# Four chained triangle blocks on one core: the norm's centring in 64x64 quarters with a third x buffer, a table load moved, a last chunk squared by tiles

## The reference

```
xn    = layer_norm(gn(x)) over the 64 channels, with scale and bias
left  = sigmoid(xn @ Wlg + blg) * (xn @ Wl + bl)      # times a mask in layers 0 and 2
right = sigmoid(xn @ Wrg + brg) * (xn @ Wr + br)
out   = einsum over one position axis: 'bikc,bjkc->bijc' (layers 0, 2) or 'bkic,bkjc->bijc' (1, 3)
gate  = sigmoid(xn @ Wog + bog)
result = (layer_norm(out) * gate) @ Wo + bo           # layers 0, 1
result = (layer_norm(out) @ Wo + bo) * gate           # layers 2, 3
```

## Time and profile before

| | us |
|---|---|
| runs: median (lowest, highest of 3) | 2204.35 (2202.63, 2204.5) |
| profiled execution: its time | 2199.82 |
| profiled execution: its span | 2197.9 |

### The profile page before, as it was taken

The page is one execution under the profiler, slowest core; times in us unless marked ns, Lnnn a source line. Parts: engine busy times, 40 slices in busy tenths (PEclk is TensorE's granted clock), DMA queues, the critical chain, the costliest instruction groups (busy, mean ns, idle before and its releaser), DMA issues. The chain is left out here.

```text
span 2197.9 us, 44344 instructions
## 1 busy us (share of the span) xinstructions
PE 1957.8 (89%) x13973; PEld 1352.7 (62%) x13980; DVE 1691.4 (77%) x2690; ACT 1589.8 (72%) x2186; POOL 623.3 (28%) x590
## 2 busy tenths in 40 slices
PE   5798979689898998989989899899998989899998
PEld 4434959555433777865633598886553357778665
DVE  6688898989588767788958897877775877677664
ACT  3588878779788655658978785776887866566676
POOL 0100828265200000026410280742871000000655
PEclk8899999999999999999999999999999999999999
DMA  9488937279788928269979973927997884663897
GB/s 394 162 264 286 281 95 212 90 290 371 256 263 261 335 77 296 87 225 398 410 229 277 273 185 127 276 57 259 402 393 225 274 305 159 219 215 125 296 350 301
DMA packets 430385, 549.47 MB, mean 250 GB/s; under 512 B 15664, under 2 KB 326960, under 8 KB 413872
## 3 DMA queue, kind: packets, MB, share of 16 engines
q1 hardware_dynamic: 428672, 538.38, 72.4%
q10 hardware_dynamic: 1584, 9.51, 1.1%
HBM read 371.67 MB, written 176.16 MB: 249 GB/s over the span
## 5 line engine op out<-in xcount | busy, mean ns | idle before, releaser
L1619 POOL TENSOR_TENSOR LR<-LR 128x512 f32<-128x512 f32 x128 | 186.6, 1475 | 523.3 <-DVE LR L1665 506.4
L823 PE MATMUL bank<-whigh,kept 128*128 128x128 f16 x2048 | 269.4, 231 | 30.5 <-DMA kept<-XH 24.6
L823 PEld LDWEIGHTS bank<-whigh,kept 128*128 128x128 f16 x2048 | 262.0, 150 | 34.7 <-issue 28.1
L1610 POOL TENSOR_TENSOR LR<-LR,sum 128x2048 f32<-128x2048 f32 x30 | 136.5, 4550 | 503.9 <-DVE LR L1427 503.9
L679 PE MATMUL bank<-LR,cen 128*128 128x512 f32 x512 | 254.8, 623 | 22.3 <-DMA LR<-XT 11.2
L823 PE MATMUL bank<-wlow,kept 128*128 128x128 f16 x2048 | 268.5, 231 | 0.0
L823 PEld LDWEIGHTS bank<-wlow,kept 128*128 128x128 f16 x2048 | 262.3, 150 | 0.0
L686 PE MATMUL bank<-LR,kst 128*128 128x512 f32 x512 | 240.9, 593 | 5.2 <-ACT LR L707 5.2
L886 POOL TENSOR_TENSOR msgs<-sigs,mask_sb 128x256 f32<-128x256 f32 x192 | 125.5, 667 | 383.8 <-ACT sigs L860 377.8
L1516 PEld LDWEIGHTS bank<-kst,LR 128*128 128x128 f32 x1024 | 151.4, 193 | 111.9 <-issue 92.5
L1528 PE MATMUL bank<-LR,wog 128*128 128x512 f16 x768 | 213.0, 387 | 6.1 <-ACT msgs L1569 5.3
(11 more groups left out here) (188 smaller groups left out, 4201.6 us busy)
## 6 DMA issues: line engine op xcount, KB each, us to landing
kept<-XH SPq DMA_DIRECT2D x128, 512.0 KB, 5.6
LR<-XT SPq DMA_DIRECT2D x64, 1024.0 KB, 9.6
kept<-XHA SPq DMA_DIRECT2D x128, 512.0 KB, 5.0
LR<-XT SPq DMA_DIRECT2D x112, 512.0 KB, 5.1
XT<-LR SPq DMA_DIRECT2D x56, 1024.0 KB, 8.8
LR<-XH SPq DMA_DIRECT2D x64, 512.0 KB, 7.0
LR<-XHA SPq DMA_DIRECT2D x64, 512.0 KB, 5.9
OS<-kept SPq DMA_DIRECT2D x12, 2048.0 KB, 7.6
```

What stands on the lines that cost most here:

```text
L823: last = pe.matmul(bank(g)[:, j * P:(j + 1) * P], tokens(h, g // 4, g % 4, j, slice(0, P)), w[:, half * P:(half + 1) * P], start=part == 0 ...
L1610: pool.tensor_tensor(v, v, token(sum2, c, C), ALU.mult).then_inc(normalized.s, 1)
L1619: pool.tensor_tensor(by_b(x_of(c), q) if end else by_token_cols(x_of(c), q), by_token(gated[t % 4]), by_token_cols(xi[c % len(xi)], q), AL ...
```

## The change

**Layout.** The two halves of the positions are no longer interleaved: partition 64 s + c. The constants, the entry's copy, the finish's output columns and the end's copy follow.

**Centring.** Each of the two 128x128 matmuls of a tile becomes two of 64x64 by 512 columns: rows by s, output partitions by half of the chunk, the four of a tile on the four quarters of PE's array. A centred tile then holds (half, channel) on the partitions and s in the columns.

**Around it.** A third x buffer (in `obuf[1]`) and loads three chunks on; three `sq` buffers instead of two, three `rs` instead of four. The halving adds 1024 to every row (a tensor-scalar add to f16, then a scalar-tensor-tensor for the remainder), so that all 64 channels are kept and POOL's constant rows go; the weights' folding subtracts the mean instead of dropping a channel. The store of a chunk is eight DMAs in layers 0 and 2, four in 1 and 3.

**Elsewhere.** The sigmoid's table is loaded in the second contraction, behind the Ln and Exp at e = 11, and no longer at the head of the finish. The finish's last chunk is squared in four instructions of 512 columns, and the sums have three more entries.

The diff, cut to its core:

```diff
         def store_xh(sp, n, part, buf, k_is_b, stored_):
-            if k_is_b:
-                for s in range(2):
-                    sp.dma_start(XH[bass.ds(n // 8, 1), 2 * s + (part ^ s), :, :, bass.ds(n % 8, 1), :]
-                                 .rearrange("o c v g f -> (o c) v (g f)"), xh_cols(buf[s::2, :], k_is_b)) \
+            for t in range(2):
+                rows = buf[C * t:C * t + C, :].rearrange("p (s f) -> p s f", s=2)
+                if k_is_b:
+                    for s in range(2):
+                        sp.dma_start(XH[bass.ds(n // 8, 1), 2 * s + (part ^ s), :, 4 * t:4 * t + 4, bass.ds(n % 8, 1), :]
+                                     .rearrange("o c v g f -> (o c) v (g f)"),
+                                     rows[:, s, :].rearrange("p (v f) -> p v f", v=4)).then_inc(stored_.s, 16)
+                else:
+                    blocks = slice(0, 4, 3) if part == 0 else slice(1, 3)
+                    sp.dma_start(XHA[blocks, :, t, bass.ds(8 * n, 8), :].rearrange("s c j a -> c s (j a)"), rows) \
                         .then_inc(stored_.s, 16)
...
+        xt_chunks = [flat[:, (4 + h) * COLS:(5 + h) * COLS] for h in range(2)] + [obuf[1][:, COLS:2 * COLS]]
...
-                        dve.tensor_copy(e_x[n % 2].rearrange("p (v c s) -> p s v c", s=2, c=C),
+                        dve.tensor_copy(e_x[n % 2].rearrange("p (v s c) -> p s v c", s=2, c=C),
...
-            sq, yc, lnv, rs = ([ar.take(GW) for _ in range(k)] for k in (2, 2, 2, 4))
+            sq, yc, lnv, rs = ([ar.take(GW) for _ in range(k)] for k in (3, 2, 2, 3))
...
+                load_xt_chunk(sp, 2, 2, k_is_b)
+                for n in range(NCH - 1):
+                    if n + 3 < from_dram:
+                        sp.wait_ge(centered.s, centered.n + 2 * n + 2)
+                        load_xt_chunk(sp, n + 3, n % 3, k_is_b)
+                    if n >= 1:
+                        store(n - 1, (n - 1) % 2)
...
                 def center(t):
...
-                    for u in range(2):
-                        at = 2 * (t % 2) + u
-                        cols = xa[h][:, at * BANK:(at + 1) * BANK] if k_is_b else \
-                            xa[h].rearrange("p (g j r) -> p j g r", g=16, j=8)[
-                                :, 4 * (at % 2):4 * (at % 2) + 4, 8 * (at // 2):8 * (at // 2) + 8, :]
-                        to = banks[t % 3][:, u * BANK:(u + 1) * BANK]
...
-                        last = pe.matmul(to, cen[:, :], cols, start=True, stop=True)
+                    for half in range(2):
+                        for s in range(2):
+                            rows = slice(C * s, C * s + C)
+                            to = banks[t % 3][C * half:C * half + C, s * BANK:(s + 1) * BANK]
...
+                            elif k_is_b:
+                                cols = xa[h][rows, (2 * half + u) * BANK:(2 * half + u + 1) * BANK]
...
+                            last = pe.matmul(to, cen[rows, rows], cols, start=True, stop=True)
                     last.then_inc(centered.s, 1)
...
-                for t in range(tiles + 1):
-                    if t < tiles:
-                        center(t)
-                    if t > 0:
-                        vary(t - 1)
+                center(0)
+                center(1)
+                for t in range(tiles):
+                    vary(t)
+                    if t + 2 < tiles:
+                        center(t + 2)
...
-                for h in range(2):
-                    pool.memset(high[h][96:P, :], X_SCALE).then_inc(rows_set.s, 1)
-                    pool.memset(low[h][96:P, :], 0.0).then_inc(rows_set.s, 1)
...
-                    dve.scalar_tensor_tensor(yc[t % 4][0:kept, :], banks[t % 3][0:kept, :], cb[0:kept, :],
-                                             rs[t % 4][0:kept, :], ALU.add, ALU.mult).then_inc(normed.s, 1)
+                    dve.scalar_tensor_tensor(yc[t % 4], banks[t % 3][:, :], cb, rs[t % 3], ALU.add, ALU.mult).then_inc(normed.s, 1)
...
-                    dve.tensor_copy(high[h][0:kept, cols], yc[t % 4][0:kept, :]).then_inc(highs_ready.s, 1)
+                    dve.tensor_scalar(to, y, X_SCALE, None, ALU.add).then_inc(highs_ready.s, 1)
                     dve.wait_ge(highs_ready.s, highs_ready.n + t + 1)
-                    dve.tensor_tensor(low[h][0:kept, cols], yc[t % 4][0:kept, :], high[h][0:kept, cols],
-                                      ALU.subtract).then_inc(lows_ready.s, 1)
+                    dve.scalar_tensor_tensor(rest, y, X_SCALE, to, ALU.add, ALU.subtract).then_inc(lows_ready.s, 1)
...
                         root(act, 0)
+                        act.preload_act_table_set("sigmoid_and_others")
...
                 def square(t):
                     c, q = divmod(t, 4)
-                    if q < 3:
-                        return
+                    if c == NCH - 1:
+                        act.wait_ge(x_ready.s, x_ready.n + t + 1)
+                        act.wait_ge(stats_taken.s, stats_taken.n + c + q)
+                        act.activation(pair_cols(squares_out[:, :], q), pair_cols(x_of(c), q), ACT.Square, bias=shift,
+                                       accum_out=stats[:, c + q, 1:2]).then_inc(stats_taken.s, 1)
+                    elif q == 3:
...
-                act.preload_act_table_set("sigmoid_and_others")
...
+    same_side = np.arange(P)[:, None] // C == np.arange(P)[None, :] // C
...
+    k[:, K_CENTER:K_CENTER + P] = np.eye(P) - same_side / C
...
+    k[:, K_MEAN:K_MEAN + P] = same_side / C
...
+    k[:C, K_DROP:K_DROP + P] = (np.arange(C)[:, None] == np.arange(P)[None, :] % C) - 1 / C
+    k[:, K_LAST:K_LAST + P] = 1 / C
```

More of the change, by code:

```diff
@@ L175, in bank @@
             return banks[i // 2][:, (i % 2) * BANK:(i % 2 + 1) * BANK]
-        loaded = [sem(f"loaded{i}") for i in range(2)]
+        loaded = [sem(f"loaded{i}") for i in range(3)]
         landed = [sem(f"landed{i}") for i in range(4)]
@@ L195, in build @@
         normed = sem("normed")
-        rows_set = sem("rows_set")
         highs_ready = sem("highs_ready")
@@ L405, in rest @@
                 for part, w in enumerate((whigh, wlow)):
-                    dve.tensor_tensor(wog[part][:, :].rearrange("p (h s) -> p h s" if late else "p (s h) -> p h s", s=2),
+                    dve.tensor_tensor(wog[part][:, :].rearrange("p (s h) -> p h s", s=2),
                                       w[:, 256:320].unsqueeze(2).broadcast_to([P, C, 2]),
@@ L418, in build @@
         ar = Arena(6 * COLS)
-        e_n = xt_chunks + [ar.take(COLS) for _ in range(2)]
+        e_n = xt_chunks[0:2] + [ar.take(COLS) for _ in range(2)]
         e_x = [ar.take(COLS) for _ in range(2)]
@@ L622, in norm @@
             cb, k_is_b = small[:, 7:8], layer["k_is_b"]
-            per, tiles = 64, 2 * NCH
-            kept = P - 2
+            per, tiles = 128 if k_is_b else 64, 2 * NCH
             @block.sync
@@ L634, in _ @@
                     sp.wait_ge(stored[h].s, stored[h].n)
[L636 to L639, removed]
                 def store_entered(c):
                     sp.dma_start(pair_chunk(XT, c // 8, c % 8), entered(c)).then_inc(stored[2].s, 16)
[L644 to L653, removed]
+                load_xt_chunk(sp, 2, 2, k_is_b)
[5 more added lines that the diff above has]
+                        store(n - 1, (n - 1) % 2)
+                    if from_dram <= n + 2 < NCH:
+                        store_entered(n + 2)
                 for h in range(2):
@@ L699, in square @@
                     act.wait_ge(centered.s, centered.n + t + 1)
[L700 to L701 removed]
+                    act.wait_ge(variance.s, variance.n + t - 2)
+                    act.activation(sq[t % 3], banks[t % 3][:, :], ACT.Square, bias=cb).then_inc(squared.s, 1)
                 def root(t):
@@ L709, in root @@
                     act.wait_ge(logged.s, logged.n + t + 1)
-                    act.wait_ge(normed.s, normed.n + t - 3)
-                    act.activation(rs[t % 4], lnv[t % 2], ACT.Exp, scale=-0.5).then_inc(rooted.s, 1)
+                    act.wait_ge(normed.s, normed.n + t - 2)
+                    act.activation(rs[t % 3], lnv[t % 2], ACT.Exp, scale=-0.5).then_inc(rooted.s, 1)
                 for h in range(4):
                     act.wait_ge(stored[h].s, stored[h].n)
-                for t in range(tiles + 1):
-                    if t < tiles:
-                        square(t)
-                    if t > 0:
-                        root(t - 1)
-            @block.gpsimd
-            def _(pool):
-                for h in range(4):
-                    pool.wait_ge(stored[h].s, stored[h].n)
-                for h in range(2):
-                    pool.memset(high[h][96:P, :], X_SCALE).then_inc(rows_set.s, 1)
-                    pool.memset(low[h][96:P, :], 0.0).then_inc(rows_set.s, 1)
+                square(0)
+                for t in range(tiles):
+                    if t + 1 < tiles:
+                        square(t + 1)
+                    root(t)
             @block.vector
```

72 lines of the change are left out of this document (32 added, 40 removed).

## The result

The changed kernel takes 2176.76 us (median of 4 runs, 2175.5 to 2179.66) where the kernel before takes 2203.65 beside it: a ratio of 0.988, 95% interval 0.9863 to 0.9897. So 27 us are saved where 45 were forecast. The profiled execution took 2175.5 (span 2173.6), 24.3 less than the one before.

What follows compares the result with a forecast made beforehand. It took a ring of waits in the norm, 7.31 of 7.44 us a pair, as the bound. Savings of 37 (norm pairs) + 6 (starts) + 1 (squares) + 1 (table load) = 45 us gave 2159 us, range 2140 to 2250.

Steps and rivals of the forecast that it cites:

- Centring: In the norm: the four quarters run together, so a centring takes 0.86 us, plus 0.18 for the change of array depth.
- the switch: In the norm on PE: changing between 128 and 64 array rows costs 0.18 us each way, at centring and variance product.
- the ring: In the norm: the loop of waits through PE, ACT and DVE for two tiles, falling from 7.31 to 6.71 us.
- Rival A: In the centring: a waiting second pass blocks the next quarter, eight passes take five pass times; 2247 us, chance 0.34.
- rival B: In the centring: only halves of the rows overlap, eight passes take four pass times; about 2204 us, chance 0.10.
- Waits for loads: In the norm: waits for x loads add 0.13 us a pair on average, kept in the forecast pair of 6.84.
- Three x buffers: In the norm: loads start one chunk earlier; alone worth at most 8 us, counted as nothing in the forecast.
- Stores: In the norms of layers 0 and 2: SP's issues take 5.9 us a pair, under 6.84, so the queue keeps up.
- Rival C: In the norm: quarters run together, but DVE's add or SP's eight stores limit pairs to 7.1-7.4 us; 2187 us, chance 0.10.
- Starts: At the norm's start in each layer: shorter first centrings at the lower clock save 1.5 us each, 6 in all.
- Squares: At the finish's last chunk: squaring by tiles on ACT lets three go earlier and saves 1 us.
- Table load: Moved from the finish's head into the contraction: ACT's wait for PE covers its 1.28 us, gaining 1 us.

Runs made afterwards that it cites:

- Experiment 3: The changed kernel with the centring as four matmuls of 128 rows x 64 columns, so only the columns are split: 2221.21 us.
- 10: The changed kernel with the two loops over the quarters exchanged, so neighbours in issue order lie on the same rows and different columns: 2174.88 us.
- experiment 7: The kernel before with the third x buffer alone: 2196.91 us, ratio 0.9968.
- experiment 2: The changed kernel with two x buffers as before, all else kept: 2226.39 us, 1.0096 of the kernel before.
- experiment 1: The changed kernel, layers 0 and 2: x chunks loaded in one DMA instead of two, stores of layer 0's entered x issued from ACT's queue: 2175.98 us.

## Why the prediction was right, and where it was not

The direction and the mechanism held, the size did not: 27 of 45 us.

*Centring*: right. 1.04 with the switch was forecast, 1.02 measured; the ring 6.71, and 6.71 is the pair in the steady parts of layers 1 and 3. That the ring comes out to the hundredth is luck in part: the variance product, 2.02 from its start to the Ln instead of 1.92, shows 0.10 of the 0.18 for the switch back, and the centring starts 1.43 after the scaling instead of 1.33, which no term held. The reason given (neighbours on different rows) was too narrow: experiments 3 and 10 show that halves of the columns overlap as well, and that the order is free. Rival A falls with the four passes at once, rival B with 1.02 instead of 1.7. Experiment 3, where PE is the bound, also bears out the price taken for a change of shape, 0.18 forecast, 0.16 and 0.19 seen.

*Waits for loads*: the 0.13 that I kept were not there with the third buffer (6.70 instead of 6.84 a pair in layers 1 and 3).

*Three x buffers*: "at most 0.13 x 62 = 8 us" is right for the kernel before, where experiment 7 gives 7.9 in the norms. As a price of this part of the change it was wrong: without it the changed kernel loses 50 us and is slower than the one before. I had noted that x loads stand behind stores, but not that x was only just in time already, 9.6 us after its buffer was free, and that a shorter pair and stores that land in 4.1 instead of 2.7 would make it late. That layers 1 and 3 "keep their four" stores said nothing of what each of them costs in the new layout.

*Halving on DVE*: right, 0.685 for the add against the 0.68 taken.

*Stores*: the step that failed. "8 x 0.63 + 2 x 0.44 = 5.9 per pair, under 6.84, so the queue keeps up, with 0.9 to spare" took an issue's price from a queue with room. In the rows above one of eight takes 5.57 / 8 = 0.70 in layer 2 and 6.75 / 8 = 0.84 in layer 0, an x load's 1.19 / 2 = 0.60 instead of 0.44, and 0.75 for a store was named as the point from which SP binds. Rival C's second half thus came true in part of two layers out of four: pairs of 7.10 and 6.94 on average, which cost (7.10 + 6.94 - 2 x 6.70) x 15.5 = 10 us against layers 1 and 3. The same norm sum as forecast is two errors that cancel.

*What no step held*: the late stores stand in front of the projection's first load. The gaps grew by 11.1 us, and nothing in the sum asked what comes next on SP's queue when the norm ends. With four stores the norms and gaps together improve by another 15 us and the kernel takes 2155.4, where I forecast 2159 by a sum in which the stores were free.

*Starts*: first centring to first Ln is 1.5, 1.7, 1.1 and 0.2 shorter, 4.5 instead of 6. *Squares*: 0 instead of 1, since the four tiles queue behind the former chunk's square (the prediction named this queue, but took off only 0.4 for it). *Table load*: 1.8 and 1.4 gained in the finishes of layers 2 and 3, 1.4 lost ahead of layer 1's, so about 1 to 2 where 1 was forecast, but the claim that ACT's wait for PE covers the load is false in layer 1.

What stays open: why eight DMAs of 128 KB hold the queue longer than four of 256 KB with the same bytes and pieces. Taking other issues off SP did not help; what an issue waits for, the profile does not show. Nor is it known why the new layout's stores land later, or how much of the 50 us of experiment 2 is theirs. Nor is it settled how much of the 4.7 us in the projections is the late loads and how much the clock.

## What to carry to other kernels

Price a DMA issue by the queue it will stand in after the change, not by its median in a queue with room; twice as many DMAs for the same bytes is a cost of its own. When a stage is shortened, look at the queue that feeds the next one: what was finished in the shadow of the stage is now in front of the next stage's first load. And a buffer that is worth 8 us in the old kernel can be worth 50 in the changed one, so a part costed at nothing has to be costed with the others made.

## What was not expected of the hardware

A matmul's pass on free columns starts while an earlier one in the code's order waits for its own (641.47, two passes within 0.02 us, columns 0, 0, 1, 1). The same store DMA's issue took 0.66 alone in its queue and 0.92 beside a transfer from another engine's queue, with SP doing nothing else (5.26 / 8 and 7.39 / 8, experiment 1). A store of 256 KB in as many pieces of the same size took 3.7 to 4.1 us to land instead of 2.7 once it read neighbouring partitions and wrote into two blocks (experiment 2).
